# Small transposes moved behind the weighing matmuls, and routed rows transposed into the other FFN bank

## The reference

```python
xn = layernorm(x)
# attention: 8 heads of 16, each split in two maps of 8
scores = einsum('bqhif,bkhif->ibhqk', q, k) * scale
atts = softmax(scores, axis=-1)
att = atts[0] - diff_weight * atts[1]
o = einsum('bhqk,bkhe->bqhe', att, v)
attn = (o * rms(o) * norm_w) @ Wo.T + bo, times (1 - diff_weight)
# FFN: 1 shared and 8 routed experts, 128 -> 256 -> 128, top 2 by sigmoid gate
out = (shared + routed) / 3
x = x + attn + out
```

## Time and profile before

| | |
|---|---|
| median of three runs | 604.8 us (603.62 to 604.98) |
| profiled execution, its own time | 604.48 us |
| its span in the trace | 602.5 us |
| mean granted TensorE clock, share of full | 0.976 |
| PE busy | 569.5 us (95%) |
| DVE busy | 470.8 us (78%) |
| ACT busy | 401.7 us (67%) |
| POOL busy | 217.4 us (36%) |

### The profile page before, as it was taken

How to read it: one execution, slowest core, us unless ns; L and a number is a source line. 1 busy time by engine, 2 the same in 40 slices (tenths; PEclk the granted TensorE clock), 3 DMA queues, 4 the chain that set the end, 5 groups by cost and what they waited for, 6 DMA issues and landing times.

```text
span 602.5 us, 13620 instructions
## 1 busy us (share of the span) xinstructions
PE 569.5 (95%) x4725; PEld 337.4 (56%) x4725; DVE 470.8 (78%) x1012; ACT 401.7 (67%) x808; POOL 217.4 (36%) x296
## 2 busy tenths in 40 slices
PE   7797999998999989999999999999999999999994
PEld 6574545554555554466655655566556656665443
DVE  4989778887888887787777787887877878877294
ACT  4363565766676756777677767777677767776682
POOL 5540053555555554033232343222433333232320
PEclk9788898999999999999999999999999999999899
DMA  5995300250116221576346834476444845430292
GB/s 162 211 183 119 103 16 14 70 136 25 37 37 147 58 79 38 148 192 201 101 128 149 247 100 140 128 196 173 141 138 122 219 146 143 123 98 14 77 302 58
DMA packets 62531, 74.07 MB, mean 123 GB/s; under 512 B 7296, under 2 KB 42496, under 8 KB 62464
## 3 DMA queue, kind: packets, MB, share of 16 engines
q1 hardware_dynamic: 57952, 64.00, 40.8%
q0 software_dynamic: 4352, 8.95, 4.6%
q10 hardware_dynamic: 160, 0.26, 0.2%
HBM read 40.08 MB, written 15.80 MB: 93 GB/s over the span
## 4 chain that ended last, share of the span: by engine, by line
PE 68%; DVE 15%; issue 6%; ACT 3%; POOL 2%; DMA 2%; SPq 2%; POOLq 0%; DVEq 0%; ACTq 0%
PE O L1163 17%; PE T L1134 10%; PE F L1203 8%; DVE rowmax L842 7%; PE F L1217 7%; PE T L1139 4%; PE F L1200 3%; PE F L1097 2%; PE F L1182 2%; DVE hid L861 2%; PE O L1124 2%; PE O L1029 1%; SPq L261 1%; DVE base L934 1%; PE F L1087 1%
## 5 line engine op out<-in xcount | busy, mean ns | idle before, releaser
L648 ACT ACTIVATE probs<-T 128x512 f32<-128x512 f32 x372 | 202.4, 596 | 107.9 <-PE T L1139 70.0
L842 DVE TENSOR_REDUCE rowmax<-S 128x1 f32<-128x512 f32 x370 | 237.9, 682 | 30.1 <-PE S L1124 27.7
L1124 PE MATMUL S<-kop,qop 32*128 32x512 f32 x370 | 140.9, 456 | 3.3 <-DVE rowmax L842 2.2
L1163 PE MATMUL O<-probs,vop 128*32 128x512 f32 x1024 | 125.5, 607 | 0.0
L482 POOL DMA_INDIRECT yt<-ysb,xst x72 | 71.0, 986 | 138.3 <-DMA yt<-ysb,xst 125.7
L1134 PE MATMUL T<-qop,kop 32*128 32x512 f32 x372 | 99.7, 500 | 1.4 <-ACT probs L648 1.0
L1139 PE MATMUL T<-mop,ones_r 2*128 2x512 f32 x372 | 78.5, 400 | 0.0
L471 POOL DMA_INDIRECT xs<-xn,slot_i x64 | 62.5, 976 | 42.9 <-DVE rowmax L842 31.0
L648 ACT ACTIVATE probs<-V 128x512 f32<-128x512 f32 x126 | 76.1, 604 | 1.8 <-PE S L1139 0.9
L1203 PEld LDWEIGHTS F<-xsT,wrt_all 128*128 128x128 f32 x576 | 67.0, 191 | 13.2 <-issue 9.4
L842 DVE TENSOR_REDUCE rowmax<-V 128x1 f32<-128x512 f32 x59 | 40.7, 689 | 43.1 <-PE S L1124 32.5
(11 more groups left out here) (168 smaller groups left out, 903.7 us busy)
## 6 DMA issues: line engine op xcount, KB each, us to landing
wrt_all<-in_wexp SPq DMA_DIRECT2D x72, 384.0 KB, 3.9
qop<-qparts SPq DMA_DIRECT2D x64, 128.0 KB
kop<-kparts SPq DMA_DIRECT2D x62, 128.0 KB
xs<-xst SPq DMA_DIRECT2D x12, 387.0 KB, 7.0
xst<-xs SPq DMA_DIRECT2D x36, 129.0 KB, 4.0
base<-in_x SPq DMA_DIRECT2D x8, 256.0 KB, 4.5
xn<-yt SPq DMA_DIRECT2D x8, 256.0 KB, 5.0
out_x<-base SPq DMA_DIRECT2D x7, 256.0 KB, 4.1
```

The source lines that it names most:

```text
L648: A(probs[:, n % NP, :], banks[e_bank[n]][:, :], ACT.Exp, scale=SCALE).then_inc(s_p, 1)
L842: V.reduce_max(rowmax[hf][:, x_map[n], c, x_row[n]:x_row[n] + 1], banks[x_bank[n]][:, :], AX).then_inc(s_mx, 1)
L1124: mm(banks[x_bank[n]][:, :], qop[b % 2][at:at + BAND, c, t * P:(t + 1) * P], kop[b % 2][at:at + BAND, c, :], start=True, stop=True, tile_p ...
L1163: last = mm(O[VW * j:VW * (j + 1), :], vop[b % 2][:, t, (4 * g + j) // MAPS, :], probs[:, n % NP, :], start=(t == 0), stop=(t == QT - 1), ...
```

## The change

Three things move. On PE, the small task of a third gap comes after `weigh` and `do_xsT` instead of before `weigh`. On ScalarE, the copy of the small task moves from the end of its pair to the front of the next one, behind `copy_O` and `copy_xsT` and ahead of the exponentials of the first gap. And `do_xsT` writes into bank F1 instead of F0, so that its claim waits for F1's last reader, and `copy_xsT` reads from there.

```diff
                 if r >= 2:
                     act.wait_ge(s_h3, tile_of(r - 2) + 1)
-                A(xsT[r % 2][:, :], F[0][:, 0:TOK], ACT.Copy).then_inc(s_xtc, 1)
+                A(xsT[r % 2][:, :], F[1][:, 0:TOK], ACT.Copy).then_inc(s_xtc, 1)
...
                 if r is not None:
                     copy_xsT(r)
+                if w == 2 and b >= 1:
+                    copy_nT(b - 1)
+                if w == 3:
+                    copy_m(2 * b + 1)
+                if w == 5 and b + 2 < BATCH:
+                    copy_q(b + 2)
+                if w == 7 and b + 1 < BATCH:
+                    copy_m(2 * (b + 1))
                 for n in exps(p, 0):
                     exp_tile(n)
...
                 for n in exps(p, 2):
                     exp_tile(n)
-                if w == 1 and b >= 1:
-                    copy_nT(b - 1)
-                if w == 2:
-                    copy_m(2 * b + 1)
-                if w == 4 and b + 2 < BATCH:
-                    copy_q(b + 2)
-                if w == 6 and b + 1 < BATCH:
-                    copy_m(2 * (b + 1))
...
             def do_xsT(r):
-                bank = F[0]
-                claim(["F0"], s_xtc, r + 1)
+                bank = F[1]
+                claim(["F1"], s_xtc, r + 1)
...
                 scores(p, 2)
+                if p < PAIRS - 1:
+                    weigh(2 * p)
+                weigh(2 * p + 1)
+                r = routed(tile_at(2 * p + 2))
+                if r is not None:
+                    do_xsT(r)
                 if w == 1 and b >= 1:
                     do_nT(b - 1)
...
                 if w == 6 and b + 1 < BATCH:
                     do_mT(2 * (b + 1))
-                if p < PAIRS - 1:
-                    weigh(2 * p)
-                weigh(2 * p + 1)
-                r = routed(tile_at(2 * p + 2))
-                if r is not None:
-                    do_xsT(r)
```

## The result

The changed kernel took 607.83 us in the median of six runs, beside 604.0 us for the kernel before in its six. The ratio is 1.0065, with a 95% interval of 1.0042 to 1.0087: slower by about 0.65%. One of the six runs (618.26 us) was in a slower state of the chip, and the ratios here leave such runs out. I had said 612.0 us, slower by 1.2%. The sign was right, and so was the stall that makes the kernel slower. The time lies in the range that I gave, but I forecast about twice the loss: against my 604.5 I had added 7.6 us, and measured are 3.8 us.

What follows compares the result with a forecast made beforehand. PE, busy 309.45 of 316 us in the routed stretch, was taken as the bound. Terms 9.9 - 5.0 + 2.1 + 0.6 = +7.6 us on 604.48 gave 612.1, stated as 612.0 us; range 607 to 616.

Steps and rivals of the forecast that it cites:

- F1's wait: End of routed pairs: `do_xsT` waits about 0.8 us until `gate_hid` has read F1; routed pairs sum to +9.9 us.
- the shared pairs: Pairs 4 to 19, without `do_xsT`: the removed wait for F0 is pure gain; this part sums to -5.0 us.
- the third part: Front of the pair: small copies now stand ahead of the first exponentials; +2.1 us for `copy_q`, +0.6 for `copy_m`.
- There is no slack: First exponentials after `copy_q`: they start 0.35 us later and six pairs pay it, +2.1 us, between 0 and 6.6.
- the task behind the transposes: End of routed pairs with a small task: 0.37 us for two transposes plus the task, 0.58 us in w = 1.
- my paragraph on the clock: Routed stretch: granted clock was 1.00, so no term; each hundredth of mean clock lost would cost up to 3.2 us.
- the later DMA of the maxima: `copy_m` about 2.5 us later feeds a DMA read in the third gap: in time by about 1 us, costed at nothing.
- A: Rival, routed pairs: the wait for F1 is hidden and the kernel gets faster, 595.5 us; chance 0.08.
- B: Rival: stalls at a pair's end are given back in the next; half absorbed gives 604 us, no change; chance 0.04.
- C: Rival, front of the pair: full `copy_q` copies and late negated maxima add 0.5 us in some twenty pairs, 616 to 620; chance 0.13.
- D: Rival: the clock falls in the routed stretch; two hundredths would give 618 us; chance 0.02.
- waits for `copy_m`: Front of the pair: `do_proj` and `do_k` claim F0 before the copy ends, 0.05 to 0.1 us; thirteen pairs, +0.6 us.

Runs made afterwards that it cites:

- the one with mixed banks: The changed kernel, but `do_xsT` uses F1 only in pairs with a small task and F0 in the others: 598.79 us, ratio 0.9897 to the kernel before.

## Why the prediction was right and where it was wrong

**Right: F1's wait.** "They now have to wait about 0.8 us, with PE's whole queue behind them." The waits on PE add up to 15.1 us (forecast 16.5), and with the bank alone changed the stretch grows by 8.66 us (forecast 8.8 for that kernel). The end of `gate_hid` did not move with the weighing, and no part of the stall was absorbed. This is shown from both sides: the bank alone makes the loss, and without it in w = 3, 5 and 7 the loss is gone.

**Right: the shared pairs.** -1.5 and -1.2 us for pairs 10 and 18 against -1.50 and -1.24 measured.

**Wrong: the third part's "There is no slack".** This is the step that failed, the term that was furthest off. I charged 0.35 us for `copy_q` in six pairs, 2.1 us, and 0.3 us came. The delay of the exponentials itself was as said. In the changed kernel's pair 37, which answers to the earlier trace rows:

```profile
373.50 0.50 PE L1134 MATMUL T<-qop,kop 32*128 32x512 f32 x2
...
374.58 1.09 ACT L648 ACTIVATE probs<-T 128x512 f32<-128x512 f32 x2
374.66 1.28 DVE L842 TENSOR_REDUCE rowmax<-S 128x1 f32<-128x512 f32 x2
375.26 0.96 PE L1134 MATMUL T<-qop,kop 32*128 32x512 f32 x2
...
376.07 0.42 PE L1124 MATMUL S<-kop,qop 32*128 32x512 f32 x1
...
376.42 2.05 PE L1203 MATMUL F<-xsT,wrt_all 128*128 128x128 f32 x16
```

The exponentials start 1.08 us into the pair, and the group of score matmuls takes 0.96 instead of 0.65 us. But `up` (L1203) starts 2.92 us into the pair (376.42 - 373.50). In the kernel before it was the same 2.92 us, 378.11 - 375.19, as these rows of its timeline show:

```profile
376.34 1.99 DVE L842 TENSOR_REDUCE rowmax<-S 128x1 f32<-128x512 f32 x3
...
377.68 0.50 PE L1124 MATMUL S<-kop,qop 32*128 32x512 f32 x1
...
378.11 0.38 PE L1203 MATMUL F<-xsT,wrt_all 128*128 128x128 f32 x1
```

The last score matmul of the gap (L1124, bank S1) starts at 377.68, well after its neighbours at 377.10, because VectorE's maxima still held S1. That wait ends last in this gap, so the score matmuls for the exponentials could come later at no cost. I had taken the first wait that I saw there for the one that ends last. Only pair 21, which has no FFN tile, pays, 0.32 us: there the matmuls of the second gap wait for the exponential itself, 0.67 instead of 0.35 us.

**Mis-sized: the task behind the transposes.** I added 0.37 us for the transposes and the small task's old cost. Directly behind one another they cost 0.27 + 0.53 (w = 1). That is 0.14 us less in w = 1, 0.17 to 0.18 in w = 4, and 0.07 to 0.10 in w = 2 and 6, some 1.9 us over 16 pairs. In w = 3 and 5 the steps were larger than forecast by up to 0.08 us, 0.5 us in eight pairs. In w = 3 `do_proj` loses 0.08 us in the first gap (I had charged 0.05), the difference falls by as much ahead of the third gap, and the step at its end is larger by as much.

**Left out: the ends.** I had costed them at nothing, and my paragraph on the clock looked at the routed stretch alone. Two pieces go with half-clock stretches outside it. These are the rows of the granted clock in the two pages, before and after, in 40 slices of the span:

```profile
PEclk9788898999999999999999999999999999999899
```

```profile
PEclk9898998999999999999999999999999999999998
```

The first piece is the -1.40 us by pair 1. The granted clock over pair 0 was 0.58 in the kernel before and 0.71 in the changed one, whose code is the same up to pair 2. In the other eight traces, again with this code, the difference at pair 1 lies between -1.18 and +0.51 us. So this is the run and not the change.

The second is a fall of 1.6 us from pair 58 to 59. In the kernel before, pair 58's weighing took 2.91 us since the clock was granted at half:

```profile
559.00:563.00 4.00, 4.00 (x21) 1.26 (x25) 0.68 (x4) 2.43 (x5) 2.98 (x5) 0.61 0.07 20
```

Over these 4 us the granted clock was 0.61 (the column after the five engines). It was 1.00 in the changed kernel (weighing 1.92 us) and also with the bank alone changed, whose code in pair 58 is that of before, and the same fall of 1.6 us is there. So the code of pair 58 does not make it. But both profiles of the kernel before have the half clock in pair 58, and none of the eight profiles of other kernels has. Whether something earlier in the kernel before brings it on, or chance did twice, these runs don't show; if it belongs to that kernel, the 1.6 us are a gain of the change that I had not seen.

After it the changed kernel loses 0.55 us where I had costed the later DMA of the maxima at nothing:

```profile
569.76 0.49 PE L1134 MATMUL T<-qop,kop 32*128 32x512 f32 x2 [0.48 <-DMA mop<-mrows]
```

Pair 59 has no FFN tile and is short. SP issues the second transfer 1.38 us into the pair, and with the 1.85 us of the earlier trace rows it lands as the third gap begins, 3.2 us into the pair in the kernel before. It is at the edge: of the seven kernels with this copy at the front of pair 59, two stood here, this one for 0.48 us and the one with mixed banks for 1.18 us, and five did not. I had worked the margin out for the long pairs only.

**The rivals.** A (hidden wait, faster) is out: the waits are real. B (absorbed) is out by the bank alone. C (the front costs more) is out: `copy_q` cost less than I had charged, and the maxima landed late in one pair only. D: the granted clock of the routed stretch stayed at 1.00, now with 22 stalls:

```profile
235.00:551.00 316.00, 300.20 (x2550) 183.84 (x2547) 242.18 (x463) 226.81 (x460) 95.20 (x126) 1.00 0.51 145
```

PE is busy for 300.20 us of the same window instead of 309.45. The oscillation that the Trainium skill tells of ("TensorE: Matmul & The Clock Gate", Part 1) is not seen with pauses of this length either.

**How it adds up.** The differences of the traces, in us:

| stretch | forecast | measured |
|---|---|---|
| start to pair 1 | 0 | -1.4 |
| pairs 2 to 21 (-5.0, three `copy_q`, four waits for `copy_m`) | -3.8 | -3.8 |
| pairs 22 to 56 | +11.4 | +8.9 |
| pairs 57 to the end | 0 | -0.5 |
| sum | +7.6 | +3.2 |

So 4.4 us are missing. 2.5 of them are in the routed pairs: 1.05 for the three `copy_q` there, and nearly all the rest (1.9 less 0.5) for the tasks behind one another and the steps of w = 3 and 5. 1.9 are at the ends, where the two half-clock pieces take 3.0 away. The stretch of pairs 2 to 21 agrees by some luck: two `copy_q` cost nothing there, and pair 4, for which I had forecast a small gain, lost 0.35 us, which I can't explain. The medians differ by 3.8 us; where in each of those runs the clock was at half, no trace shows.

## What to carry to other kernels

When a task changes its bank, look for who reads the new bank last and when that reader ends, not only for whether the old wait goes away: here one claim in 36 places cost 1.25% of the kernel, more than the reordering that it came with gained. If a wait for another engine can't be avoided, put work that doesn't need it in front: with the same banks, the order weighing, small task, transposes gave 0.9829 of the time of before, where weighing, transposes, small task gave 0.9897. And before a delay is charged to the critical path, list all waits of that gap and take the one that ends last.

## What the runs showed of the hardware

Two profiles of the same program on different chips differed by up to 5.5 us by the end of the first 21 pairs, and by 0.14 us over the 36 pairs after them; where they grew apart, in pairs 7 to 21, the granted clock was 1.00 in both. Half-clock stretches of PE outside the dense part came at different places in different traces: in pair 58 in both profiles of the kernel before (weighing 2.91 us, and 3.44 in the second, at a granted clock of 0.61 and 0.57 over 4 us) and in no other (1.92 us with the same code there), in pair 21 in two other kernels (0.81 and 0.73 over the pair). PE took over a PSUM bank 0.05 to 0.06 us after VectorE's last read of it ended. Where single microseconds matter, the steady stretch of a trace is the better balance; the medians carry this noise.
